# A macaron block (routed experts, diagonal state space, routed experts) on one core: a new middle stage and routing with one fp16 number

## The chip, the cores and the metric

The kernel runs on one NeuronCore of a Trainium2 chip. TensorE multiplies matrices into PSUM; VectorE, ScalarE and GpSimd do the elementwise work; SyncE issues most of the DMAs. TensorE's clock has two levels, 2.4 and 1.2 GHz, and the profile shows the granted one as a share of full speed. The metric is device microseconds of one execution.

## The reference

```python
# x: 4096 tokens of 256 numbers
x = x + 0.5 * ffn(layernorm(x))
x = x + ssm(layernorm(x))
x = x + 0.5 * ffn(layernorm(x))

def ffn(x):                          # 8 experts, hidden size 1024
    p = softmax(x @ Wr)              # the largest p chooses the expert
    h = gelu(x @ W1[e] + b1[e])      # erf form
    return max(p) * (h @ W2[e] + b2[e])

def ssm(u):                          # 128 complex states, diagonal
    h_t = a_disc * h_{t-1} + B_disc @ u_t
    return Re(C @ h_t)
```

## The kernel before

Everything stays on one core, and the engines are joined by semaphores; each engine's program is written out in its order. There are five stages.

Entry: x comes in as eight chunks of 512 tokens (4 tiles of 128 rows), row statistics are taken (`entry_stats`), the rows are transposed by TensorE and multiplied by the centred routing weights to give the logits. At the same time the 16 expert weight matrices are loaded and each is split into two fp16 parts; ScalarE sums the magnitudes (`row_sums`) and makes the high part, VectorE the scales (`weight_scales`) and the low part (`low_part`). Between these, VectorE's program has the steps of the first routing.

Routing (`route_*`): from the logits, VectorE finds each token's expert (`route_choose`), TensorE counts tokens before each one, VectorE turns this into a slot in a list sorted by expert (`route_count`), in tiles of 128 tokens of one expert, 39 tiles at most. `route_tiles` makes for each token a row over the tiles, once with the tile's start (GpSimd's `tile_starts`) and once with its partition, and `route_rows` a row over the 128 slots (32 operations of 128 columns). TensorE multiplies one with the other, which puts the number of the token into its slot, and `route_sorted` makes three index lists of it (`sorti`). `route_weigh` gives the largest probability, which goes to DRAM with mean and deviation as one record a token.

Experts (`ffn`, run twice): for each of 39 tiles GpSimd gathers rows and records by index, ScalarE normalises them (`norm`), TensorE transposes (`turn_tile`), VectorE splits them into a high and a low fp16 part (`split_x`), TensorE does the first product in three terms (`product1`), ScalarE does GELU, VectorE splits the result (`split_h`), TensorE does the second product (`product2`), VectorE scales it and adds x (`result`), and GpSimd scatters the rows.

Middle (state space): a loop over the eight chunks, with up to five of them in SBUF (XS). VectorE takes the statistics of the rows (`row_stats`, L580 to L586), GpSimd makes the inverse deviation, ScalarE normalises (L430), TensorE transposes (L976) and multiplies into the states (L1134), ScalarE copies the result (L543). The recurrence is a real scan after a rotation: VectorE multiplies by the cosine (L913), GpSimd by the sine (L414), VectorE runs two scans (L917, L920), and four one-column operations (L927 to L930) carry the state to the next chunk. GpSimd rotates back (L397, L399, L403), TensorE multiplies out of the states (L1114), and VectorE adds y to the rows (L942). Then for the next routing the new rows have statistics, a normalisation, transposes and logits of their own (L982), which trail the chunk loop: the logits of chunk c are copied LATE = 4 iterations later (L908).

Last come the second routing and the second expert stage. Two places of the code before:

```python
posi -> q1 = (iota_b == tile_b)                    # L749
dve.tensor_scalar(sval[:, :, 1, :], q1, part[:], None, ALU.mult)   # L752
...
last = dve.tensor_scalar(onerow[:, j, :], iota_b[:], slot_f[:, j:j + 1], None, ALU.is_equal)   # L757
```

## Time and profile before

| | |
|---|---|
| median of 3 runs | 737.88 us (733.58 to 748.28) |
| span of the profiled execution | 743.5 us |
| TensorE matmuls busy | 589.5 us (79%) |
| VectorE busy | 531.1 us (71%) |
| ScalarE busy | 396.8 us (53%) |
| GpSimd busy | 330.0 us (44%) |
| mean granted TensorE clock | 0.869 |

The profile is of one execution: the table gives for each engine the time in which it had an instruction in work. The only own time that the profiled execution has is its span, from the first to the last instruction; it lies within the spread of the runs and 5.6 us above their median. PE is TensorE's matmul, PEld its weight load, DVE VectorE, ACT ScalarE, POOL GpSimd, SP SyncE.

### The profile page before, as it was taken

How to read it: one execution, taken by the hardware profiler on the slowest of the kernel's cores; microseconds unless marked ns; L12 is line 12 of the kernel's file. 1: busy time of each engine (PE TensorE's matmuls, PEld its weight loads, DVE VectorE, ACT ScalarE, POOL GpSimd, SP SyncE). 2: the span in 40 equal slices, each digit the busy share in tenths (PEclk: the TensorE clock that was granted, in tenths of full speed). 3: DMA queues.
4: the chain of work that ended last, by engine and by line, in shares of the span. 5: the costliest groups of instructions: out<-in, count | busy, mean ns of one | idle time of the engine just before them, and what ended most of it. 6: DMA issues, size and time to landing. Idle time of an engine off the chain costs nothing.

```text
span 743.5 us, 18466 instructions
## 1 busy us (share of the span) xinstructions
PE 589.5 (79%) x6396; PEld 518.0 (70%) x6396; DVE 531.1 (71%) x1204; ACT 396.8 (53%) x879; POOL 330.0 (44%) x310
## 2 busy tenths in 40 slices
PE   5960149999999899994477878139999999999997
PEld 5950138998888787893245657129998778988886
DVE  5869967778886775784499993927776666766675
ACT  4877846565554555552336653107555546546463
POOL 0031183555545453531477881162555454554532
PEclk9555559999999999998658895558999999999999
DMA  8993031111111111113102211030111111111210
GB/s 276 374 375 122 5 99 31 40 45 43 49 45 38 35 51 37 38 30 99 51 29 90 80 57 57 1 103 19 44 51 44 36 50 36 45 41 36 50 36 2
DMA packets 34872, 51.86 MB, mean 70 GB/s; under 512 B 6747, under 2 KB 27933, under 8 KB 34528
## 3 DMA queue, kind: packets, MB, share of 16 engines
q1 hardware_dynamic: 24800, 31.90, 12.6%
q0 software_dynamic: 9984, 18.79, 9.0%
q8 instruction: 55, 0.90, 0.5%
q14 instruction: 33, 0.27, 0.1%
HBM read 37.95 MB, written 14.55 MB: 71 GB/s over the span
## 4 chain that ended last, share of the span: by engine, by line
PE 68%; DVE 18%; issue 7%; DMA 3%; ACT 2%; POOL 1%; SPq 1%; ACTq 0%; POOLq 0%; DVEq 0%
PE bank L1065 31%; PE bank L1082 9%; PE bank L1083 9%; PE bank L1084 9%; PE bank L982 4%; PE bank L1041 3%; DVE stats L580 3%; DVE weights_arena L613 2%; PE bank L976 2%; DMA weights_arena<-L_attn_u 2%; DVE weights_arena L920 1%; DVE weights_arena L757 1%; DVE weights_arena L917 1%; DVE weights_arena L942 1%; DVE ev L927 1%
## 5 line engine op out<-in xcount | busy, mean ns | idle before, releaser
L519 ACT ACTIVATE weights_arena<-bank,b1t,inv 128x128 f32<-128x128 f32 x624 | 228.4, 467 | 211.2 <-PE bank L1065 161.2
L1065 PE MATMUL bank<-weights_arena 128*128 128x128 f16 x3744 | 239.2, 222 | 23.5 <-issue 17.5
L1065 PEld LDWEIGHTS bank<-weights_arena 128*128 x3744 | 220.6, 99 | 39.8 <-issue 37.0
L1082 PE MATMUL bank<-weights_arena 128*128 x624 | 170.2, 273 | 1.2 <-issue 1.0
L1083 PE MATMUL bank<-weights_arena 128*128 x624 | 170.1, 273 | 1.3 <-issue 1.1
L1084 PE MATMUL bank<-weights_arena 128*128 x624 | 170.1, 273 | 0.9 <-issue 0.6
L816 DVE TENSOR_SCALAR weights_arena<-weights_arena,hscale 128x512 f16<-128x512 f32 x156 | 76.8, 492 | 83.6 <-ACT weights_arena L519 77.4
L819 DVE SCALAR_TENSOR_TENSOR weights_arena<-weights_arena,hscale 128x512 f16<-128x512 f32 x156 | 117.3, 752 | 5.6
L375 POOL DMA_INDIRECT recf<-records,sorti x78 | 81.4, 1043 | 23.8 <-issue 23.8
L381 POOL DMA_INDIRECT out<-weights_arena,sorti x39 | 39.5, 1013 | 112.7 <-DVE weights_arena L835 99.8
L381 POOL DMA_INDIRECT x_after_ffn<-weights_arena,sorti x39 | 40.6, 1040 | 105.3 <-DVE weights_arena L835 95.8
L1084 PEld LDWEIGHTS bank<-weights_arena 128*128 128x128 f16 x624 | 61.0, 98 | 10.5 <-issue 3.5
L1083 PEld LDWEIGHTS bank<-weights_arena 128*128 128x128 f16 x624 | 61.1, 98 | 9.0 <-issue 2.9
L1082 PEld LDWEIGHTS bank<-weights_arena 128*128 128x128 f16 x624 | 61.0, 98 | 8.9 <-issue 2.4
L803 DVE TENSOR_SCALAR weights_arena<-bank,xscale 128x256 f16<-128x256 f32 x78 | 37.7, 484 | 38.8 <-issue 17.2
L504 ACT ACTIVATE weights_arena<-weights_arena,recf 128x256 f32<-128x256 f32 x78 | 48.7, 626 | 30.1 <-DMA recf<-records,sorti 28.1
L375 POOL DMA_INDIRECT weights_arena<-L_attn_u,sorti x39 | 44.0, 1128 | 30.3 <-DVE sorti L788 18.8
L976 PE MATMUL bank<-ident,weights_arena 128*128 128x128 f32 x192 | 37.0, 358 | 19.6 <-ACT weights_arena L430 18.1
L976 PEld LDWEIGHTS bank<-ident,weights_arena 128*128 128x128 f32 x192 | 32.2, 195 | 27.5 <-ACT weights_arena L430 22.5
L832 DVE SCALAR_TENSOR_TENSOR weights_arena<-bank,inv,weights_arena 128x256 f32<-128x256 f32 x78 | 37.4, 479 | 19.1 <-PE bank L1084 9.5
L375 POOL DMA_INDIRECT weights_arena<-x_after_ssm,sorti x39 | 41.0, 1050 | 20.3 <-issue 11.6
L1041 PE MATMUL bank<-ident,weights_arena 128*128 128x128 f32 x156 | 31.4, 283 | 15.0 <-ACT weights_arena L504 13.1
(181 smaller groups left out, 702.0 us busy)
## 6 DMA issues: line engine op xcount, KB each, us to landing
weights_arena<-L_ffn_W SPq DMA_DIRECT2D x16, 1024.0 KB, 12.6
weights_arena<-L_attn_u SPq DMA_DIRECT2D x8, 512.0 KB, 9.9
weights_arena<-x_after_ffn SPq DMA_DIRECT2D x8, 512.0 KB, 4.8
x_after_ssm<-weights_arena SPq DMA_DIRECT2D x8, 512.0 KB, 3.1
weights_arena<-L_ffn_b SPq DMA_DIRECT2D x2, 1024.0 KB, 4.4
recf<-records,sorti POOLq DMA_INDIRECT x78
weights_arena<-L_attn_u,sorti POOLq DMA_INDIRECT x39
x_after_ffn<-weights_arena,sorti POOLq DMA_INDIRECT x39
```

The source lines that it names most:

```text
L375: pool.indirect_dma_start(to, None, source, bass.IndirectOffsetOnAxis(ap=sorti[:, q, index:index + 1].bitcast(U32), axis=0)).then_inc(s["g ...
L381: pool.indirect_dma_start(dst, bass.IndirectOffsetOnAxis(ap=sorti[:, q, 2:3].bitcast(U32), axis=0), og[q % 2], None, bounds_check=T - 1, o ...
L504: act.activation(xng[q % 2], xg[q % RING], ACT.Identity, bias=recf[:, q % RING, 0:1], scale=recf[:, q % RING, 1:2]).then_inc(s["xn"], 1)
L519: last = act.activation(hb[q % 2][:, f, :], src, ACT.Gelu, bias=b1t[:, bass.ds(e * FC + f, 1)], scale=inv1[:, bass.ds(e, 1)])
L816: dve.tensor_scalar(hs[q % 2][:, 0, f, :], hb[q % 2][:, f, :], sc, None, ALU.mult) \
L819: dve.scalar_tensor_tensor(hs[q % 2][:, 1, f, :], hb[q % 2][:, f, :], sc, hs[q % 2][:, 0, f, :], ALU.mult, ALU.subtract).then_inc(s["hspli ...
L976: last = pe.transpose(banks[d][:, i * P:(i + 1) * P], src[:, i, d * P:(d + 1) * P], ident[:])
L1041: last = pe.transpose(bank[6 + q % 2][:, d * P:(d + 1) * P], xng[q % 2][:, d * P:(d + 1) * P], ident[:])
L1065: last = pe.matmul(acc[:, f * P:(f + 1) * P], weights[wpart * DC + d], xts[q % 2][:, xpart, d, :], start=(n == 0), stop=(n == 5))
L1082: pe.matmul(acc, hs[q % 2][:, 0, f, :], high, start=(f == 0), stop=False)
L1083: pe.matmul(acc, hs[q % 2][:, 0, f, :], low, start=False, stop=False)
L1084: last = pe.matmul(acc, hs[q % 2][:, 1, f, :], high, start=False, stop=(f == FC - 1))
```

## The change

The middle stage and the routing are written anew; the expert stage changes in three places.

- The first expert stage takes mean and variance of each result row on VectorE and stores them behind the row: rows of 258 numbers (RW) in place of 256 in the buffer between.
- All eight chunks are loaded into SBUF at once. GpSimd makes the deviations in three batches, of chunk 0, of 1 and 2, and of 3 to 7; VectorE's loop begins when all three are ready.
- No products on GpSimd: VectorE multiplies both halves in one operation of 1024 columns, out of PSUM, runs both scans in place, and rotates back in one operation and a sum.
- Logits by linearity: the rows behind the state space are x + y, so the logits are those of the normalised x times its deviation, plus those of y, for which the matrix out of the states has nine more columns (eight experts and the mean). Normalisation, transposes and copies of the new rows go. ScalarE takes the new variance as a sum of squares; GpSimd makes its inverse square root at the end, for all 32 columns, and `route_odds` multiplies by it.
- Routing with one fp16 number: the number of the token, shifted by 2048 and never 0, in place of two bf16 numbers. One operation of 1280 elements multiplies it in, and `route_rows` is four operations of 1024, whose operands are laid out in pairs. The list for the first gather is released ahead of the other two.
- In the expert stage the high part of x is made by ScalarE, in the order GELU of q, high x of q+2, norm of q+3; TensorE's second product waits for `o_chain` in place of `o`.
- TensorE has extra products that nobody reads (`idle`) at the start of the middle and around the routing.

Not shown below: the layout of the buffers, the fp16 constants (token numbers), the nine columns of `ct` made at entry with one small product, the dropped operation and new order in `route_count`, and most of the removed lines.

```diff
-LATE = 4
-XS = 5
+PAIRS = 2
+RW = D + 2
...
-    x1_dram = nc.dram_tensor("x_after_ffn1", [T, D], F32, kind="Internal").ap()
+    x1_dram = nc.dram_tensor("x_after_ffn1", [T, RW], F32, kind="Internal").ap()
...
-            for c in range(XS):
-                sp.dma_start(xs[c], x1_chunks[c]).then_inc(sx[c], 16)
+            for c in range(NC):
+                sp.dma_start(xs[:, c * CT:(c + 1) * CT, :], x1_chunks[c]).then_inc(s_load[c], 16)
             for c in range(NC):
...
+            for first, last in BATCHES:
+                for c in range(first, last):
+                    pool.wait_ge(s_load[c], 16)
+                of = slice(first * CT, last * CT)
+                pool.tensor_scalar(nb[:, of], xs[:, of, D], -1.0, None, ALU.mult)
+                chain.link(pool.tensor_scalar(var1[:, of], xs[:, of, D + 1], EPS, None, ALU.add))
+                chain.link(pool.tensor_tensor(rs[:, of], var1[:, of], mhalf[:, of], ALU.pow))
+                chain.link(pool.tensor_tensor(sd[:, of], rs[:, of], var1[:, of], ALU.mult))
+                pool.tensor_tensor(nb[:, of], nb[:, of], rs[:, of], ALU.mult).then_inc(s_nb, 1)
+            pool.wait_ge(s_sq, NC)
+            chain.link(pool.tensor_scalar(m2[:], m2[:], 1.0 / D, EPS, ALU.mult, ALU.add))
+            chain.link(pool.tensor_tensor(rstd, m2[:], mhalf[:], ALU.pow))
+            pool.tensor_tensor(shift, nmean[:], rstd, ALU.mult).then_inc(s_nb2, 1)
...
+                def high_x(q):
+                    e = experts[q] = act.value_load(eid[0:1, q:q + 1], min_val=0, max_val=E - 1)
+                    act.wait_ge(s["turned"], q + 1)
+                    if q >= 2:
+                        act.wait_ge(s["xt"], q - 1)
+                        act.wait_ge(s["m1"], q * 2 - 2)
+                    src = bank[6 + q % 2][:, 0:DC * P].rearrange("p (c t) -> p c t", c=DC)
+                    act.activation(xts[q % 2][:, 0], src, ACT.Copy, scale=xscale[:, bass.ds(e, 1)]).then_inc(s["xt_hi"], 1)
                 norm(0)
                 norm(1)
+                high_x(0)
+                norm(2)
+                high_x(1)
                 for q in range(NT):
...
                         last.then_inc(s["gelu"], 1)
+                    if q + 2 < NT:
+                        high_x(q + 2)
+                    if q + 3 < NT:
+                        norm(q + 3)
...
+            def normalise(c):
+                act.wait_ge(s_nb, 1 + sum(first <= c for first, last in BATCHES[1:]))
                 if c >= 2:
+                    act.wait_ge(s_ut, c - 1)
+                for i in range(CT):
+                    j = c * CT + i
+                    act.activation(uns[c % 2][:, i, :], xs[:, j, 0:D], ACT.Identity, bias=nb[:, j:j + 1],
+                                   scale=rs[:, j:j + 1]).then_inc(s_un, 1)
+            def turned(c):
+                act.wait_ge(s_ut, c + 1)
                 if c >= 2:
+                    act.wait_ge(s_lg, c - 1)
+                for d in range(DC):
+                    last = act.copy(uts[c % 2][:, d, :], bank[d])
+                last.then_inc(s_uts, 1)
+            def squares(c):
+                act.wait_ge(s_x2, c + 1)
+                act.wait_ge(s_nm, c + 1)
+                if c >= 1:
+                    act.wait_ge(s_sq, c)
+                for i in range(CT):
+                    j = c * CT + i
+                    last = act.activation(dumps[i], xs[:, j, 0:D], ACT.Square, bias=nmean[:, j:j + 1],
+                                          accum_out=m2[:, j:j + 1])
+                last.then_inc(s_sq, 1)
...
+            def route_odds(ph):
+                s = S[ph]
+                dve.wait_ge(s["top"], 1)
+                dve.wait_ge(a_nb if ph == 1 else s_nb2, 1)
+                dve.tensor_tensor(je(rt[0]), je(rt[0]), over_e(rstd), ALU.mult).then_inc(s["diff"], 1)
...
+                dve.tensor_scalar(place_i[:, 0], posi, P - 1, None, ALU.bitwise_and)
+                link(dve.tensor_scalar(place_i[:, 1], posi, 7, None, ALU.arith_shift_right))
+                link(dve.tensor_copy(place_h, place_i.unsqueeze(3).to_broadcast([P, 2, NJ, PAIRS])))
+                pairs = lambda a: a.rearrange("p j (k t) -> p j k t", t=PAIRS)
+                link(dve.tensor_tensor(
+                    pairs(q1), iota_h[:, 0:NTE].rearrange("p (k t) -> p k t", t=PAIRS).unsqueeze(1)
+                    .to_broadcast([P, NJ, NTE // PAIRS, PAIRS]),
+                    place_h[:, 1].unsqueeze(2).to_broadcast([P, NJ, NTE // PAIRS, PAIRS]), ALU.is_equal))
+                dve.tensor_tensor(pairs(sval), pairs(q1),
+                                  token_h[:].unsqueeze(2).to_broadcast([P, NJ, NTE // PAIRS, PAIRS]), ALU.mult) \
+                    .then_inc(S[ph]["vals"], 1)
...
+                of = slice(GR * g, GR * g + GR)
+                dve.tensor_tensor(
+                    onerow[:, of, :].rearrange("p j (k t) -> p j k t", t=PAIRS),
+                    iota_h[:].rearrange("p (k t) -> p k t", t=PAIRS).unsqueeze(1).to_broadcast([P, GR, P // PAIRS, PAIRS]),
+                    place_h[:, 0, of, :].unsqueeze(2).to_broadcast([P, GR, P // PAIRS, PAIRS]), ALU.is_equal) \
+                    .then_inc(S[ph]["row"], 1)
...
+                number = bank[1][:, 0:NT]
+                upper, empty, token, high = (view(12928 + NTE * k, NT) for k in range(4))
+                dve.tensor_scalar(empty, number, 0.0, BIG, ALU.is_equal, ALU.mult)
+                link(dve.tensor_scalar(upper, number, 0.0, None, ALU.is_gt))
+                link(dve.tensor_tensor(token, number, upper, ALU.subtract))
+                link(dve.scalar_tensor_tensor(token, token, float(T // 2), empty, ALU.add, ALU.add))
+                dve.tensor_scalar(sorti[:, :, 0], token, float(T - 1), None, ALU.min).then_inc(s["sorted_sb"], 1)
+                dve.wait_ge(s["sorted_sb"], 1)
+                dve.tensor_scalar(sorti[:, :, 1], sorti[:, :, 0], P - 1, 5, ALU.bitwise_and, ALU.arith_shift_left)
+                dve.tensor_copy(sorti[:, :, 2], token)
+                link(dve.tensor_scalar(high.bitcast(I32), sorti[:, :, 0], 7, None, ALU.arith_shift_right))
+                dve.tensor_tensor(sorti[:, :, 1], sorti[:, :, 1], high.bitcast(I32), ALU.add).then_inc(s["sorted_all"], 1)
...
                     dve.wait_ge(s["o_chain"], q + 1)
+                    last = dve.scalar_tensor_tensor(o, o, recf[:, q % RING, 2:3], xg[q % RING], ALU.mult, ALU.add)
+                    if ph == 1:
+                        link(last)
+                        link(dve.bn_stats(stats[:, q % 2, :], o))
+                        last = dve.bn_aggr(og[q % 2][:, D:D + 2], stats[:, q % 2, :])
+                    last.then_inc(s["o"], 1)
...
+            def logits_of(c):
+                dve.wait_ge(s_y, c + 1)
+                of = slice(c * CT, (c + 1) * CT)
+                dve.scalar_tensor_tensor(nmean[:, of], ybanks[:, :, D + E], -1.0, xs[:, of, D], ALU.mult, ALU.subtract) \
+                    .then_inc(s_nm, 1)
+                link(dve.tensor_tensor(lpart[:], ybanks[:, :, D + NB:D + NB + E],
+                                       sd[:, of].unsqueeze(2).to_broadcast([P, CT, E]), ALU.mult))
+                dve.tensor_tensor(logits[:, of, :], lpart[:], ybanks[:, :, D:D + E], ALU.add).then_inc(s_lg, 1)
+            def add_y(c):
+                rows = xs[:, c * CT:(c + 1) * CT, 0:D]
+                dve.tensor_tensor(rows, rows, ybanks[:, :, 0:D], ALU.add).then_inc(s_x2, 1)
...
+            dve.wait_ge(s_nb, len(BATCHES))
+            for c in range(NC):
+                dve.wait_ge(s_g, c + 1)
+                dve.tensor_tensor(zz, turn[:], both(bank[2]), ALU.mult).then_inc(s_mod, 1)
+                dve.wait_ge(s_mod, c + 1)
+                for part_of in range(2):
+                    scan = dve.tensor_tensor_scan(zz[:, part_of, :], rho[:].to_broadcast([P, CH]), zz[:, part_of, :],
+                                                  state[:, part_of:part_of + 1], ALU.mult, ALU.add)
+                scan.then_inc(s_scan, 1)
+                if c >= 1:
+                    logits_of(c - 1)
+                    add_y(c - 1)
+                dve.wait_ge(s_scan, c + 1)
+                if c + 1 < NC:
                     dve.tensor_tensor(ev[:, 20:21], zi, sl, ALU.mult)
                     link(dve.tensor_tensor(ev[:, 21:22], zr, sl, ALU.mult))
...
+                    link(dve.scalar_tensor_tensor(state[:, 1:2], zi, cl, ev[:, 21:22], ALU.mult, ALU.subtract))
+                link(dve.tensor_tensor(zb, zz, back[:], ALU.mult))
+                if c >= 2:
+                    dve.wait_ge(s_y, c - 1)
+                dve.tensor_tensor(hr[c % 2], zb[:, 0, :], zb[:, 1, :], ALU.add).then_inc(s_hr, 1)
+            logits_of(NC - 1)
+            dve.wait_ge(s_lg, NC)
             route_choose(2)
+            add_y(NC - 1)
             route_count(2)
             route_tiles(2)
             for g in range(NJ // GR):
                 route_rows(2, g)
...
+                    for j in range(GR * g, GR * g + GR):
+                        last = pe.matmul(bank[1][:, 0:NTE], onerow[:, j, :], sval[:, j, :], start=(j == 0), stop=(j == NJ - 1))
                     last.then_inc(s["rowused"], 1)
...
+            def turn_chunk(c):
+                if c >= 1:
+                    pe.wait_ge(s_uts, c)
+                for i in range(CT):
+                    pe.wait_ge(s_un, c * CT + i + 1)
+                    for d in range(DC):
+                        last = pe.transpose(bank[d][:, i * P:(i + 1) * P], uns[c % 2][:, i, d * P:(d + 1) * P], ident[:])
+                last.then_inc(s_ut, 1)
+            def into_states(c):
+                pe.wait_ge(s_uts, c + 1)
+                if c >= 1:
+                    pe.wait_ge(s_mod, c)
+                for d in range(DC):
+                    last = pe.matmul(bank[2], bt[:, d, :], uts[c % 2][:, d, :], start=(d == 0), stop=(d == DC - 1))
+                last.then_inc(s_g, 1)
+            def out_of_states(c):
+                if c >= 1:
+                    pe.wait_ge(s_lg, c)
+                    pe.wait_ge(s_x2, c)
+                for i in range(CT):
+                    for d in range(DC):
+                        pe.matmul(ybanks[:, i, D + NB:D + NB + E], uts[c % 2][:, d, i * P:(i + 1) * P], wrc[:, d, 0:E],
+                                  start=(d == 0), stop=(d == DC - 1))
+                pe.wait_ge(s_hr, c + 1)
+                for i in range(CT):
+                    last = pe.matmul(ybanks[:, i, 0:D + NB], hr[c % 2][:, i * P:(i + 1) * P], ct[:], start=True, stop=True)
+                last.then_inc(s_y, 1)
+            idle(10, CH)
+            turn_chunk(0)
+            into_states(0)
+            turn_chunk(1)
+            for c in range(NC):
                 if c + 1 < NC:
...
+            idle(8)
             route(2)
             ffn(2)
```

## Rows read from the trace of the kernel before

**Rows 1.** Busy time by stage: stretch in us, length, engines, granted clock, DMA share, GB/s.

```profile
104.00:343.00 239.00, 226.41 (x2882) 205.12 (x2882) 172.93 (x350) 133.11 (x351) 113.57 (x110) 0.99 0.14 40
343.00:364.00 21.00, 6.38 (x16) 3.81 (x17) 4.81 (x22) 5.70 (x11) 3.62 (x6) 0.60 0.38 125
364.00:452.00 88.00, 66.38 (x297) 47.91 (x296) 82.43 (x211) 44.36 (x85) 66.37 (x58) 0.81 0.19 62
452.00:464.00 12.00, 9.33 (x44) 8.60 (x42) 1.31 (x11) 4.22 (x8) 1.22 (x2) 0.54 0.10 35
464.00:494.00 30.00, 5.43 (x40) 3.02 (x41) 21.16 (x75) 3.10 (x5) 8.63 (x8) 0.50 0.14 51
494.00:743.50 249.50, 229.85 (x2882) 207.25 (x2880) 165.85 (x310) 131.86 (x349) 112.86 (x111) 0.98 0.13 38
```

**Rows 2.** Timeline of one iteration of the middle: start us, duration us, engine, line.

```profile
394.99 1.96 PE L1114 MATMUL bank<-ct,weights_arena 128*128 128x256 f32 x8 [1.87 <-DVE weights_arena L942]
...
396.88 0.68 DVE L913 TENSOR_TENSOR weights_arena<-weights_arena,turn 128x512 f32<-128x512 f32 x1
...
397.31 1.09 PE L976 MATMUL bank<-ident,weights_arena 128*128 128x128 f32 x8 [0.36 <-ACT weights_arena L430]
...
398.24 1.85 PE L982 MATMUL bank<-wr,weights_arena 128*128 128x8 f32 x16
398.44 1.07 ACT L530 COPY weights_arena<-bank 128x512 f32<-128x512 f32 x2 [1.18 <-PE bank L976]
...
398.80 1.26 DVE L920 TENSOR_TENSOR_SCAN weights_arena<-rho,state,weights_arena 128x512 f32<-128x512 f32 x1
398.96 2.16 POOL L397 TENSOR_TENSOR weights_arena<-weights_arena,back 128x512 f32<-128x512 f32 x1
...
399.95 1.96 PE L1134 MATMUL bank<-weights_arena,bt 128*128 128x512 f32 x4
400.16 0.98 DVE L927 TENSOR_TENSOR ev<-weights_arena,turn 128x1 f32<-128x1 f32 x1
...
401.06 0.15 DVE L928 TENSOR_TENSOR ev<-weights_arena,turn 128x1 f32<-128x1 f32 x1
...
404.41 1.28 DVE L942 TENSOR_TENSOR weights_arena<-weights_arena,bank 128x512 f32<-128x512 f32 x2
```

**Rows 3.** The lower clock: one timeline row, and a stretch of two microseconds.

```profile
379.79 3.78 PE L1134 MATMUL bank<-weights_arena,bt 128*128 128x512 f32 x4 [1.16 <-ACT weights_arena L530]
...
404.00:406.00 2.00, 0.16 (x1) 0.19 (x2) 1.93 (x9) 0.00 (x0) 1.27 (x3) 0.78 0.00 0
```

**Rows 4.** Load of the middle's rows, first statistics, and GpSimd's power at entry.

```profile
350.00:352.00 2.00, 0.00 (x0) 0.00 (x0) 1.20 (x4) 0.00 (x0) 0.00 (x0) 0.50 1.07 367
...
350.80 1.40 DVE L580 BATCH_NORM_STATS2 stats<-weights_arena 128x6 f32<-128x256 f32 x4 [6.91 <-DMA weights_arena<-x_after_ffn]
...
36.39 7.50 POOL L353 TENSOR_TENSOR records<-weights_arena,mhalf 128x32 f32<-128x32 f32 x1 [19.39 <-DVE weights_arena L865]
```

**Rows 5.** Timeline of the second routing, VectorE.

```profile
473.21 1.49 DVE L749 TENSOR_TENSOR weights_arena<-iota_b,weights_arena 128x1280 bf16<-128x1280 bf16 x1
474.74 2.72 DVE L752 TENSOR_SCALAR weights_arena<-weights_arena,part 128x1280 bf16<-128x1280 bf16 x1
...
477.38 5.29 DVE L757 TENSOR_SCALAR weights_arena<-iota_b,weights_arena 128x128 bf16<-128x128 bf16 x32
...
485.40 0.18 DVE L788 TENSOR_SCALAR sorti<-weights_arena 128x39 int32<-128x39 f32 x1
```

**Rows 6.** Waits at entry (60 to 104): total us, times, longest.

```profile
ACT weights_arena L459 <- DVE wscale L606: 7.2, 3, 3.3
```

**Rows 7.** Waits in the first experts (130 to 340), and two rows of their timeline.

```profile
PE bank L1065 <- DVE weights_arena L805: 1.8, 2, 1.5
...
303.03 2.90 ACT L519 ACTIVATE weights_arena<-bank,b1t,inv 128x128 f32<-128x128 f32 x8 [3.74 <-PE bank L1065]
...
312.26 0.94 PE L1065 MATMUL bank<-weights_arena 128*128 128x128 f16 x14
```

384 lines of the change are left out of this document (109 added, 275 removed).

## The prediction

> **What bounds the kernel now.** The span is 743.5 us, the median of the three runs 737.9 (733.6 to 748.3), so I subtract from 743.5 and take the 5.6 us between span and median off at the end. I read the stretches by stage first [rows 1]. The two expert stages (104 to 343 and 494 to 743.5) have TensorE busy 226 of 239 and 230 of 249.5 us at the high clock: TensorE sets them. The middle stage, from 343 until the logits are complete at 464, is 121 us, and the second routing, until the first product at 494, is 30. From 364 to 452 VectorE is busy 82 of 88 us while TensorE has 66 and ScalarE 44: eight iterations, one per chunk, of 11 us. After it come 12 us in which TensorE works alone through two late chunks of transposes and logits, because they trail by LATE = 4. Then I followed one iteration in the timeline [rows 2]. VectorE's one-column products cost 0.98 us (L927) and 0.15 (L928): the long one starts at 400.16 and ends when GpSimd's product L397, begun at 398.96, has ended (401.12). So two of VectorE's four state operations (L927, L929) wait about a microsecond each for GpSimd. In the routing I look at what follows what: TensorE and ScalarE are nearly idle, VectorE goes from one operation to the next, and the clock is at its lower level.
>
> **The iteration of the middle, anew.** VectorE per chunk, at the durations of [rows 2]: multiply with PSUM, 1024 columns, 1.2 (L942 takes 1.28 for two of 512); two scans 2.5 (twice L920's 1.26); three short ones for mean and logits 0.5 (each like L928 with its wait); adding y 1.2 (as L942); four state operations 0.65 without GpSimd; the backward product of 1024 columns 1.25 and the sum of 512 0.65 (L913: 0.68 for 512). Sum 7.95, with the waits between them 8.1, against 11. Gone are both statistics (2 x 2 us: L580 and what follows it) and the two waits for GpSimd; GpSimd's products come in.
> But the change also ties a ring. The copy of chunk c+2 out of PSUM (ScalarE, 1.07, L530) now waits for the logits of chunk c, since TensorE's logits read that buffer. Behind it on TensorE, in order: into states 1.96 (L1134), transposes 1.09 (L976), eight logit products 0.93 (half of L982's 1.85), y 2.03 (L1114's 1.96 for 265 columns in place of 256), then VectorE's 0.5. With 0.3 for handing over that makes 7.9 us at the high clock: just hidden under 8.1. At the low clock the same terms are 3.78 (L1134 in [rows 3]) and twice the others: 13.3 us, longer than the old iteration. The old clock fell in the gaps (404 to 406: 0.78) though TensorE was busy 66 of 88 us, and its mean was 0.81, that is 38% of the time low. TensorE's new share is 6.0 of 8.1 us, as full as before (7.9 of 11), with a gap of some 2 us in each iteration. Bounds 8.1 and 13.3; mixed by time (62% and 38%), 9.5 us. As a ring at the low clock keeps TensorE busy 11.5 of 13.3 us, which ought to raise the clock again, I take 8.9.
>
> **The start of the middle.** The last tile of the first expert stage gains a row statistic behind its result (L580: 0.35 a row, plus aggregate and waits): +0.6 until its scatter. The first chunk, which VectorE had at 350.80, comes at 351.4; the other seven of 528 KB, 3.7 MB, take 10.1 at the 367 GB/s of the old load [rows 4]: complete at 361.5. SyncE issues all eight in a row, and its stores stand behind them; the first of these is wanted 20 us later. I keep up to 370 for the high end, as rows of 1032 bytes move at a rate that no row shows. GpSimd's third batch needs all of them: pow costs 7.50 us for 32 columns (L353), 0.234 each, so 4.7 for 20 columns, plus four short operations with waits, 1.2: about 367 to 368. VectorE now waits for this batch before its first multiply (the old loop began at 364); behind that wait stand all of its chunk work, and behind that the second product into the states. TensorE's ten idle products after the last tile (5 us at most) end before the first transposes can come; they hide in the load. First multiply 368, first iteration without logits 6.1, six at 8.9: the last begins at 427.5; 7.4 until its sum, y at 2 to 3.9, logits 0.5: 438.4 against 464. **The middle gives 25.5 us.** The tail is where most is won: the old logits came some 25 us after the last chunk's multiply, the new ones by 11.
>
> The Trainium skill (DMA: Bandwidth & Descriptors, How a descriptor splits into AXI transactions) says that a transfer not starting on a 256-byte boundary also fetches the bytes below its start. A row of 1032 bytes would then fetch 128 bytes more on average, and the estimate of the seven chunks' load by this page is 11.4 us for 10.1. No row of before shows such a transfer.
>
> **The routing.** From 464 to the sorted list at 485.6 [rows 5] it takes 21.7 us. Choose stays; y's last add (1.2) now stands between choice and counts, of which 0.8 was spare: +0.4. Count loses one 256-column operation: -0.5. In tiles, L752 took 2.72 us for 1280 elements, beside GpSimd's product for the tile starts; both go. The two new operations over 1280 fp16 elements take L749's 1.49 each, or about 0.8 if pairs of 16-bit elements pass two at a time (the same slope halved, above the 0.15 of L928). Tiles: 5.2 before, 3.9 or 2.5 after. Rows: 32 operations in 5.29 before, four of 1024 elements after, 1.2 or 0.7 each: 4.8 or 2.8. Odds +0.45; sorted lists -0.1 to the first gather (its other indices, 0.7, hide behind that gather's issue). A new wait: the odds need the variances. ScalarE's last squares (four of about 0.6) start behind y's add, then GpSimd takes 0.3 + 7.5 + 0.3, ready 15 us after the logits; VectorE is there after 13.5 in the fast case, 16.9 in the slow one. Behind the wait stand odds, owners, weights and the sorted list. So 18.5 or 20.6 for 21.7. No row shows a two-operand 16-bit operation with both inputs in steps of one (L749 repeats one of them), so I keep both ends. I take the fast one, as L757 already handles 128 16-bit elements in 0.165 us, where L749's slope would give 0.28: **-3.2**. On GpSimd the gathers now stand behind the variances (ready at 15 us), before the sorted list at 18.5 that they need anyway.
> The Trainium skill (VectorE: DVE Perf Modes, the perf-mode tier table) gives tensor_tensor two 16-bit elements a cycle with unit steps and one otherwise; L749 at 1.49 fits the latter, and its rule makes the routing 18.5, without it 20.6.
>
> **Entry.** In the first routing the same VectorE operations stand in the way of the weight scales: ScalarE waited 7.2 us for L606 in three waits, the longest 3.3 [rows 6]; tiles stand before one of them and rows before the next. The savings on VectorE (0.5 + 1.3 to 2.7 + 0.5 to 2.5) come out there as far as these idle times reach: 2 to 5, I take **-3**. The new constants and the extra product for the readout fall before the second x chunks land, in VectorE's idle time.
>
> **Expert stages.** High x moves from VectorE (0.48) to ScalarE, which is busy 133 of 239 us; the statistics add 0.45 and two waits on VectorE in the first stage (173 of 239). With it go the waits for transposes and products and the register load. ScalarE now makes it behind GELU of q, and norm q+3 is queued behind it. A tile takes 6.1 us (239 / 39). GELU of one tile ran from 303.03 to 305.93, and TensorE began the first product of the tile two later at 312.26 [rows 7]. High x at 305.93 takes 0.5; VectorE's low part at worst comes behind the second half of the split of h, the result and its statistics, at 309.3: 2.9 us to spare. TensorE waited for L805 only 1.8 us in all of 130 to 340 [rows 7]. Nothing, then; range -4 to +4 over both. At each start high x now stands behind the second norm: +0.2.
>
> **Sum.** -25.5 - 3.2 - 3 + 0.4 for the two starts: 31.3 off 743.5 is 712.2, less 5.6: **706 us**, 4.3% faster. A measurement of this kernel tells about 2% from no change.
>
> **Rivals.**
> A, the clock stays up in the loop: 8.1 an iteration, 5 us less, with entry at its best 2 more and the load at its earliest: 697. For it: TensorE's gaps shrink from up to 3 us to 2; against it: the old loop was as full and fell.
> B, the ring at the low clock is the bound for most of the loop: 13.3 for six iterations is 26 more, 732; for half of them 719. For it the old mean of 0.81, against it that a bound TensorE is a busy one. At the high end this is no change by 2%.
> C, the first multiply waits for slow rows of 1032 bytes or for pow beside VectorE: +3 to +10, 709 to 716.
> D, slower: the hand-over of x in the experts. ScalarE's high x sits behind GELU, TensorE's next first product behind it. It costs nothing until the 2.9 us to spare are used; beyond that each microsecond is paid on 78 tiles. At 1.0 over, 706 + 78 = 784; from 0.4 over the kernel is slower than before, from 0.6 by over 2%. For it only that first tiles have no lead; against it [rows 7] and ScalarE's 106 idle us.
> E, the multiplies without GpSimd don't lose the wait in L927 (it was something else): two microseconds more for seven iterations, 720. The times of L397 speak against it.
>
> **How the numbers follow.** Forecast 0.56 (698 to 715), A 0.14, C 0.10, B at half 0.09, B in full 0.06, E 0.02, D 0.03. The range 692 to 724 holds the forecast, A, C, E and B at half: it leaves out D, full B and the ends of the expert stages' uncertainty. Faster by over 2% means below 723: all but D, B in full and a part of B at half and C: 0.88; same 0.09; slower 0.03.
>
> **What would show it.** Right: L913's successor every 8 to 9.5 us, all state operations at 0.15 to 0.2, first multiply near 368, logits complete near 438, scan-to-logit tail of 11, the 1280-element multiplies at 0.8 and the 1024-element compares at 0.7, expert stages of 239 and 249. Wrong: iterations of 11 to 13 with TensorE continuously busy (B), a first multiply after 371 (C), TensorE waiting for low x in the experts (D), a wait before the odds of more than 2 us.

## The result, and the profile after

The kernel after takes 681.9 us (median of four runs, 676.3 to 684.2), the kernel before 736.4 beside it (734 to 748): ratio 0.923, 95% interval 0.917 to 0.929. I had forecast 706, in a range that ended at 692. The profiled execution has a span of 679.9 us and took 681.7.

First the stages, as in [rows 1] (stretch, length, busy us and count of PE, weight loads, VectorE, ScalarE and GpSimd, granted clock, DMA share, GB/s). The six stretches are: first experts; last product to first multiply; the loop; its tail to the logits; routing; second experts.

```profile
100.00:332.50 232.50, 223.67 (x2881) 206.86 (x2881) 178.75 (x387) 149.96 (x389) 109.59 (x109) 0.99 0.15 41
332.50:357.00 24.50, 15.96 (x44) 7.31 (x41) 1.60 (x5) 8.14 (x16) 11.04 (x17) 0.83 0.54 173
357.00:413.40 56.40, 44.53 (x226) 31.81 (x226) 51.50 (x87) 26.39 (x73) 0.00 (x0) 0.92 0.16 56
413.40:424.80 11.40, 9.25 (x51) 7.96 (x52) 7.43 (x13) 3.85 (x16) 0.00 (x0) 0.85 0.14 48
424.80:450.00 25.20, 12.78 (x106) 10.69 (x104) 16.47 (x48) 5.65 (x14) 13.14 (x10) 0.82 0.25 82
450.00:680.00 230.00, 222.01 (x2882) 208.13 (x2882) 150.71 (x272) 147.24 (x387) 107.81 (x111) 0.98 0.15 41
```

From span to span 63.6 us are gone. Taking each stage from the start of its first product to that of its last three, by the instruction rows: 4.1 before the first product, 5.7 in the first experts (238.2 to 232.5), 33.8 in middle and second routing (151.6 to 117.8), 19.8 in the second experts (243.9 to 224.1). My sum had 31.3 in all and nothing in the experts.

One iteration on VectorE, in answer to [rows 2]. The four state operations (L926 to L929) take 0.15 to 0.22, with no long one among them. VectorE waits for y (L901), 1.13 here and about 0.4 later. The multiplies (L915) follow one another by 6.3, 8.6, 8.9 and then 8.2 us.

```profile
371.86 1.22 DVE L915 TENSOR_TENSOR weights_arena<-turn,banks 128x1024 f32<-128x1024 f32 x1 [0.88 <-PE banks L1119]
373.12 2.46 DVE L918 TENSOR_TENSOR_SCAN weights_arena<-rho,state,weights_arena 128x512 f32<-128x512 f32 x2
376.71 0.16 DVE L901 SCALAR_TENSOR_TENSOR nmean<-banks,weights_arena 128x4 f32<-128x4 f32 x1 [1.13 <-PE banks L1133]
...
378.24 0.15 DVE L926 TENSOR_TENSOR ev<-weights_arena,turn 128x1 f32<-128x1 f32 x1
378.31 0.15 DVE L927 TENSOR_TENSOR ev<-weights_arena,turn 128x1 f32<-128x1 f32 x1
...
380.75 1.22 DVE L915 TENSOR_TENSOR weights_arena<-turn,banks 128x1024 f32<-128x1024 f32 x1
```

The start of the middle, as in [rows 4]: GpSimd has the last load at 352.06, and its power of 20 columns takes 3.56 where I had 4.7. The first multiply follows at 356.98.

```profile
352.06 0.29 POOL L377 TENSOR_SCALAR nb<-weights_arena 128x20 f32<-128x20 f32 x1 [4.60 <-DMA weights_arena<-x_after_ffn]
352.42 0.28 POOL L378 TENSOR_SCALAR var<-weights_arena 128x20 f32<-128x20 f32 x1
352.78 3.56 POOL L379 TENSOR_TENSOR rs<-var,mhalf 128x20 f32<-128x20 f32 x1
```

The second routing, as in [rows 5]: 0.83 and 0.82 for the two operations over 1280 elements, 2.56 for all rows, and L698 behind them without an idle time in brackets, so nothing waits for the variances.

```profile
433.64 0.83 DVE L729 TENSOR_TENSOR weights_arena<-iota_h,weights_arena 128x1280 f16<-128x1280 f16 x1
434.50 0.82 DVE L733 TENSOR_TENSOR weights_arena<-weights_arena,token_h 128x1280 f16<-128x1280 f16 x1
435.25 2.56 DVE L740 TENSOR_TENSOR weights_arena<-iota_h,weights_arena 128x1024 f16<-128x1024 f16 x4
437.73 0.41 DVE L698 TENSOR_TENSOR weights_arena<-weights_arena,records 128x256 f32<-128x256 f32 x1
```

And the tail, still partly at the lower clock [rows 3]: the last chunk's logit products and y.

```profile
414.60 2.03 PE L1133 MATMUL banks<-ct,weights_arena 128*128 128x265 f32 x8
418.78 2.17 PE L1129 MATMUL banks<-wrc,weights_arena 128*128 128x8 f32 x16 [2.15 <-DVE weights_arena L910]
420.80 3.46 PE L1133 MATMUL banks<-ct,weights_arena 128*128 128x265 f32 x8
```

### The profile page after: what moved, and what is told of

Read it like the earlier page. It is cut to its first block, busy times and chain, and to the rows that moved or that the text cites. A ratio compares the mean times of both kernels' runs of the same rounds, so it can differ in the third digit from the quotient of the medians.

```text
span 679.9 us, 18383 instructions
## 1 busy us (share of the span) xinstructions
PE 576.7 (85%) x6428; PEld 518.4 (76%) x6428; DVE 483.6 (71%) x1015; ACT 416.1 (61%) x965; POOL 262.7 (39%) x263
## 4 chain that ended last, share of the span: by engine, by line
PE 69%; DVE 11%; issue 11%; DMA 3%; POOL 2%; ACT 1%; SPq 1%; DVEq 1%; ACTq 0%; POOLq 0%
PE banks L1060 30%; PE banks L1079 9%; PE banks L1077 9%; PE banks L1078 9%; PE banks L1036 2%; PE banks L1133 2%; PE banks L1119 2%; PE banks L1129 2%; DMA weights_arena<-x_after_ffn 1%; POOL records L336 1%; DVE weights_arena L918 1%; PE banks L965 1%; PE banks L993 1%; DVE weights_arena L573 1%; SPq L312 1%
## 5 line engine op out<-in xcount | busy, mean ns | idle before, releaser
L490 ACT ACTIVATE weights_arena<-banks,b1t,inv 128x128 f32<-128x128 f32 x624 | 226.2, 468 | 44.1 <-PE banks L1060 24.5
L1060 PE MATMUL banks<-weights_arena 128*128 128x128 f16 x3744 | 236.3, 222 | 12.8 <-issue 9.0
L1060 PEld LDWEIGHTS banks<-weights_arena 128*128 x3744 | 221.6, 99 | 23.0 <-issue 19.2
L1077 PE MATMUL banks<-weights_arena 128*128 x624 | 170.6, 273 | 0.0
L1078 PE MATMUL banks<-weights_arena 128*128 x624 | 170.5, 273 | 0.0
L1079 PE MATMUL banks<-weights_arena 128*128 x624 | 170.5, 273 | 0.0
L475 ACT ACTIVATE weights_arena<-banks,xscale 128x256 f16<-128x256 f32 x78 | 37.0, 474 | 110.0 <-PE banks L1036 74.8
L791 DVE SCALAR_TENSOR_TENSOR weights_arena<-banks,xscale,weights_arena 128x256 f16<-128x256 f32 x78 | 37.7, 484 | 45.8 <-issue 30.8
L1079 PEld LDWEIGHTS banks<-weights_arena 128*128 128x128 f16 x624 | 61.2, 98 | 7.3
L1077 PEld LDWEIGHTS banks<-weights_arena 128*128 128x128 f16 x624 | 61.2, 98 | 6.6
L1078 PEld LDWEIGHTS banks<-weights_arena 128*128 128x128 f16 x624 | 61.2, 98 | 6.4
L818 DVE SCALAR_TENSOR_TENSOR weights_arena<-banks,inv,weights_arena 128x256 f32<-128x256 f32 x78 | 37.5, 480 | 13.7 <-PE banks L1079 10.8
L594 DVE SCALAR_TENSOR_TENSOR weights_arena<-weights_arena,wscale 128x2048 f16<-128x2048 f32 x16 | 37.4, 2345 | 5.5 <-ACT weights_arena L417 5.4
L1036 PE MATMUL banks<-ident,weights_arena 128*128 128x128 f32 x156 | 30.7, 280 | 11.0 <-ACT weights_arena L462 9.9
```

Of the source, the lines that this page charges most:

```text
L490: last = act.activation(hb[q % 2][:, f, :], src, ACT.Gelu, bias=b1t[:, bass.ds(e * FC + f, 1)], scale=inv1[:, bass.ds(e, 1)])
L791: dve.scalar_tensor_tensor(xts[q % 2][:, 1], src, sc, xts[q % 2][:, 0], ALU.mult, ALU.subtract) \
L1036: last = pe.transpose(bank[6 + q % 2][:, d * P:(d + 1) * P], xng[q % 2][:, d * P:(d + 1) * P], ident[:])
L1060: last = pe.matmul(acc[:, f * P:(f + 1) * P], weights[wpart * DC + d], xts[q % 2][:, xpart, d, :], start=(n == 0), stop=(n == 5))
L1077: pe.matmul(acc, hs[q % 2][:, 0, f, :], high, start=(f == 0), stop=False)
L1078: pe.matmul(acc, hs[q % 2][:, 0, f, :], low, start=False, stop=False)
```

## The experiments

Each set of kernels ran on another chip, and the kernel before ran beside each: 723, 743, 738, 701 and 702 us. So a ratio to before compares within a chip, and the stages below, of one profiled execution each, help to explain it. The executions of e5 and e12 took 5 and 7 us more than the medians of their kernels. For each profiled execution: before's median on its chip; first product; first experts; last product to the first of the second stage; second experts. In brackets are TensorE's gaps: between two products of one half tile (24 of the first product, 12 of the second), where neither waits for a semaphore, the distance beyond the usual 0.056 or 0.109 us, where that is over 0.12, summed from the instruction rows.

```
                 before  first   experts 1     middle+   experts 2
                         product               routing
before             736   104.0  238.2 (15.4)   151.6   243.9 (18.1)
after              736    99.9  232.5 (13.2)   117.8   224.1 ( 2.7)
e1_experts         723   105.0  232.7 ( 8.5)   152.2   222.2 ( 2.0)
e2_experts_back    723   100.1  237.7 ( 7.6)   117.3   221.6 ( 3.0)
e3_norm_order      723   104.1  228.6 ( 7.7)   151.9   224.8 ( 4.2)
e4_no_idle         723    99.7  228.0 ( 8.7)   118.0   225.5 ( 3.1)
e5_before_again    743   105.6  240.4 (13.8)   154.1   240.8 (14.6)
e6_after_again     743    97.6  232.2 (13.0)   118.0   231.0 ( 8.4)
e7_unpaired        743   103.2  231.6 (13.3)   121.3   227.7 ( 6.3)
e8_early           743    97.5  231.8 (13.1)   111.8   225.5 ( 3.4)
e9_experts2        738   105.0  245.1 (19.3)   151.9   226.4 ( 4.1)
e10_norm2          738   105.6  233.8 (11.4)   154.2   234.9 ( 9.8)
e11_back2          738    97.5  238.8 ( 9.0)   117.3   245.5 (17.4)
e12_pad            738   103.2  242.4 (15.5)   151.7   242.0 (18.6)
e13_fewer          701   105.4  219.8 ( 0  )   153.3   216.2 ( 0  )
e14_more           701    99.9  219.6 ( 0  )   120.5   216.9 ( 0  )
e15_high_x         701    97.6  233.8 ( 0  )   115.1   215.8 ( 0  )
e16_best           701    99.6  219.0 ( 0  )   109.0   217.2 ( 0  )
e17_fewer2         702   105.5  219.6 ( 0  )   153.7   215.9 ( 0  )
e18_more2          702   105.5  219.3 ( 0  )   156.2   216.3 ( 0  )
```

**The expert stages' edits alone, and put back.** e1 and e9 are the same kernel, the kernel before with this edit (`high_x`, ScalarE's split, is defined as in the change above):

```diff
                 norm(1)
+                high_x(0)
+                norm(2)
+                high_x(1)
                 for q in range(NT):
-                    if q + 2 < NT:
-                        norm(q + 2)
 ...
                         last.then_inc(s["gelu"], 1)
+                    if q + 2 < NT:
+                        high_x(q + 2)
+                    if q + 3 < NT:
+                        norm(q + 3)
 ...
-                    dve.tensor_scalar(xts[q % 2][:, 0], src, sc, None, ALU.mult).then_inc(s["xt_hi"], 1)
 ...
-                        pe.wait_ge(s["o"], q - 1)
+                        pe.wait_ge(s["o_chain"], q - 1)
```

e2 and e11 are the kernel after with this diff reversed.

> The kernel before with the expert stages' edits of the change alone: high x on ScalarE behind GELU of q, norm of q+3 behind it, the second product waiting for VectorE's first of two operations on the result. Theory S (the unforeseen 24 us of the two expert stages come from these edits): the stages fall from 238 and 250 to about 233 and 231, the time by 20 to 24 us, to about 714. Rival R (they come from elsewhere: the clock at which the second stage starts, the code of the other stages, the data layout): at most 4 us of the stages move, 732 to 738.

> The kernel before with the expert stages' edits of the change alone, a second time. On the chip where before takes 722 us it brought 0.5%, the expert stages being near 233 and 222 us with or without it. On the chips where before takes 736 to 743, its expert stages have 14 to 18 us each of gaps between products that wait for no semaphore (in after: 13 and 3 to 8). Theory I (such gaps are TensorE's supply of instructions, tied to a place in the program and to the chip, not to the order of ScalarE's and VectorE's work): on such a chip the edit alone leaves the gaps of before in place, gain under 1.5%. Theory S (the late split takes TensorE's lead and so makes it feel the supply): the gaps or their cost fall, gain 2.5 to 3.3%.

> The kernel after with its expert stages put back: high x on VectorE, norm of q+2 ahead of GELU of q, the second product waiting for the finished result. Theory S: about 20 to 24 us more than after, 702 to 706, the second stage back near 250. Rival R: within 4 us of after, 678 to 686. If the row statistics behind the result hurt when they stand ahead of the product's wait, the first stage alone would be longer than 238.

> The kernel after with its expert stages' orders put back, a second time. Theory I: the ratio to before stays where the middle, the routing and the position of the code put it, within 1% of after's 0.922. Theory S: 0.95 or more, the second stage near 240.

Edits alone: 0.9947 of before (0.990 to 1.000) on the chip of 723, 0.9926 (0.988 to 0.997) on that of 738. Put back in after: 0.948 (0.945 to 0.952), 7.8 us above e4 on the same chip, and 0.951 (0.942 to 0.961), against 0.923 and 0.922 for after itself on other chips. The second stages of the chips at 736 to 743 are the clear reading: with the old order 243.9, 240.8, 242.0 and 245.5 us, with the new one 224.1, 231.0, 227.7, 225.5 and 226.4. The edit is worth 10 to 20 us in that stage there, in the kernel before too. But the whole of e9 gains only 5 us on its chip, and its first stage, 245.1, gives some of the rest back (two tiles of 12.0 and 10.8 us, with gaps of 3.9 and 3.8). On the chip of 723 the second stage is 222 to 226 in either order. Where ScalarE waited in the second stage (total, times, longest): first GELU in before and in e11_back2, then high x (L475) and GELU (L490) in after, then GELU in e13_fewer (old order, chip of 701):

```profile
ACT weights_arena L519 <- PE bank L1065: 78.2, 32, 4.0
ACT weights_arena L519 <- remote: 29.8, 11, 7.6
```

```profile
ACT weights_arena L477 <- PE banks L1047: 78.5, 33, 3.8
ACT weights_arena L477 <- remote: 31.1, 11, 7.5
```

```profile
ACT weights_arena L475 <- PE banks L1036: 33.5, 23, 2.3
ACT weights_arena L475 <- remote: 29.0, 13, 2.5
ACT weights_arena L490 <- remote: 6.8, 1, 6.8
ACT weights_arena L490 <- PE banks L1060: 4.3, 5, 2.4
```

```profile
ACT weights_arena L519 <- PE bank L1065: 83.6, 39, 3.9
```

The waits for the product are the ordinary lead of ScalarE; those put down to "remote" follow no product that had just ended. At GELU there are 11 of them with the old order, one with the new, none on the chip without gaps. They don't vanish with the new order: 13 of them, 29.0 us, now stand at high x, which ScalarE makes two tiles ahead. So the edit may pay because a late start now falls where a tile has time to spare; no run shows that, nor which of the three parts of the edit does it.

**The norm's order alone, and the place of the code.** e3 and e10 move only `norm(q + 2)` from ahead of GELU of q to `norm(q + 3)` behind it, in the kernel before. e12 adds to before, behind its first `ffn(1)` on TensorE,

```diff
+            for _ in range(24):
+                pe.matmul(bank[2][:, 0:P], ident[:], turn[:, 0, 0:P], start=True, stop=True)
```

> The kernel before with one thing changed: ScalarE normalises tile q+3 behind GELU of tile q, where it normalised q+2 ahead of it. Theory S1 (a late GELU is what costs, because a norm that waits for its gather or transposes stands ahead of it): most of the 20 us, 716 to 720. Theory S2 (VectorE's load is what costs, and high x must leave it): less than 5 us, 731 to 738.

> The kernel before with norm of q+3 behind GELU of q, a second time. Its TensorE program is that of before, instruction for instruction. Theory I: on a chip where before takes 736 to 743 the same gaps stand at the same tiles as in before (stage 2: 14, 17, 21, 28, 32) and the gain is under 1%. Theory S: tile times fall to 5.5 to 5.9 us and the gain is 2 to 3%.

> The kernel before with 24 idle products (48 weight loads and 48 products in TensorE's program) behind the first expert stage, where TensorE waits some 15 us for its next work, so that they cost nothing by themselves; they move all later code of TensorE by some 100 instructions. Theory I: the first expert stage is as before; in the second the gaps stand at other tiles, and their sum may go either way (by up to 12 us). Rival: the gaps of the second stage stand at the same tiles, so the place of TensorE's code is not what sets them.

The norm's order: 0.997 (0.994 to 1.000) and 1.002 (0.998 to 1.007), nothing. The profiled execution on the chip of 738 has a shorter second stage (234.9), but it was among the fastest three of ten, and the median shows no gain. The shifted code: 1.000 (0.994 to 1.005); long tiles stand at 14, 17 and 21 of the second stage as in before, others have moved. That speaks against the place of TensorE's code as their cause.

**Both kernels again on one chip.**

> The kernel before itself, unchanged, profiled on the chip of this job. In the job before this one its median was 723 us where the first comparison had 736, and two kernels with other orders in the expert stages stood at 720 to 722. Theory N (the unforeseen gain of the expert stages is no effect of the edits: the same instructions of before take a different time there from one chip to the next): its two expert stages are near 230 and 225 here, as in those two kernels, where the profile shown had 238 and 244. Theory S (the old order is slower by itself): 238 and 244 again. Where this program is slow, tiles of 5.6 us alternate with tiles of over 6.

> The kernel after itself, unchanged, on the same chip. Middle stage and second routing together, last product to first, 118 us as in its profile; expert stages about 228 to 232 and 222 to 225. Theory N: 676 to 682, ratio to before 0.935 to 0.95 in place of 0.923. Theory S: ratio 0.923 again.

Before 743.5, after 685.4, ratio 0.922 (0.915 to 0.930): the first result repeats. Theory N fell on this chip: 240.4 and 240.8. (On the chip of 723 it held, as e2 and e4 show for the second stage: 221.6 with the old order, 225.5 with the new.)

**Idle products.** e4 deletes the four `idle(...)` calls of after.

> The kernel after without TensorE's idle products, at the start and end of the middle stage and in the second routing. My reading of after: the 8.8 us of idle products after the first expert stage end before the loads have come, so they delay nothing; without them the first iterations, the tail and the first tiles of the second expert stage run at the low clock: 3 to 8 us more, 685 to 690. Rival: they bring nothing, since the clock falls while the first multiply is awaited anyway: within 2 us. Rival R's form for the expert stage: the second stage loses its gain of 19 us, 700.

0.935 (0.931 to 0.939), 678.7 us, so not the 3 to 8 us more that I expected. After itself was not timed on this chip, but middle and routing are 118.0 in its profile too: idle products bring nothing that can be seen where they stand. In both kernels the first multiply follows GpSimd's last batch, so a faster first product into the states can't show.

**Pairs.** e7 changes one line of after.

```diff
-PAIRS = 2
+PAIRS = 1
```

> The kernel after with PAIRS = 1: the fp16 operands of the routing are repeated element by element and no longer in pairs, nothing else. Theory: pairs are what lets VectorE pass two a cycle. Then the two operations over 1280 elements go from 0.83 to about 1.5 and the rows from 2.5 to 4.3 each four; per routing 1.3 + 1.8 = 3.1 or more, in the second all of it on the path, in the first most of it in front of the weight scales: 4 to 7 us more than after. Rival: the layout makes no difference to the rate: within 1 us.

0.934 (0.927 to 0.941), 6.4 us more than after on the same chip. By the profiles it is 5.6 more at entry and 3.3 more in the routing, and 3.9 less in the experts, which the edit doesn't touch. The same operations as above:

```profile
436.21 1.49 DVE L729 TENSOR_TENSOR weights_arena<-iota_h,weights_arena 128x1280 f16<-128x1280 f16 x1
437.74 1.49 DVE L733 TENSOR_TENSOR weights_arena<-weights_arena,token_h 128x1280 f16<-128x1280 f16 x1
439.15 4.69 DVE L740 TENSOR_TENSOR weights_arena<-iota_h,weights_arena 128x1024 f16<-128x1024 f16 x4
```

**An earlier start of the loop, and a version that beats both.** e8 moves a wait of after; e16 is e8 with idle products where the clock was low.

```diff
-            dve.wait_ge(s_nb, len(BATCHES))
 ...
             def logits_of(c):
+                dve.wait_ge(s_nb, 1 + sum(first <= c for first, last in BATCHES[1:]))
```

```diff
-            idle(10, CH)
+            idle(13, CH)
 ...
             def out_of_states(c):
+                if c == NC - 1:
+                    pe.wait_ge(s_mod, NC)
+                    idle(10)
```

> The kernel after, with VectorE's one wait for all three batches of the row scales taken from ahead of the first multiply and put, batch by batch, ahead of the logits that read them. In after the first multiply stands at 357.0, while the first product into the states is ready about 10 us earlier. Theory L (this wait is worth its length): the first multiply comes at about 347, the loop ends 7 to 10 us earlier, 672 to 675 where after has 680 to 682. Rival P (GpSimd's pow and VectorE slow one another, or the ring of chunk 3 waits for its load and scales anyway): the early iterations take 2 to 4 us longer and the gain is 2 us or less.

> The kernel after with VectorE's early start of e8_early, with 13 idle products in place of 10 ahead of the middle stage (so that they end where the first transposes can begin) and ten more ahead of the last chunk's products, where the clock is low in after: into the states 1.4 us, logits and y of the last chunk up to 3 us sooner than in e8_early. 668 to 674, ratio 0.905 to 0.91. Rival: the clock stays low in these places whatever is put into the gaps: the same as e8_early, 0.911.

e8: 674.9 us, 0.911 (0.904 to 0.919), 10.5 us faster than after on the same chip, 6.2 of them in the middle. The rest lies in the second experts (225.5 for 231.0), which the edit doesn't touch. Its first multiply no longer waits for GpSimd; first after, then e8:

```profile
356.98 1.22 DVE L915 TENSOR_TENSOR weights_arena<-turn,banks 128x1024 f32<-128x1024 f32 x1 [22.29 <-POOL nb L381]
```

```profile
347.73 1.22 DVE L915 TENSOR_TENSOR weights_arena<-turn,banks 128x1024 f32<-128x1024 f32 x1 [16.08 <-PE banks L1119]
```

e16: 650.8 us, 0.928 (0.923 to 0.932), on the chip where before takes 701, so its expected ratio, made for the other chips, can't be compared. Middle and routing are 109.0, 2.8 less than e8's on another chip: 1.4 less before the first multiply and 3.1 less behind the last, but 1.7 more in the loop between. The first product into the states and the tail now run at the higher clock (1.98 where after had 3.78; y 2.04 where it had 3.46):

```profile
333.68 1.98 PE L1119 MATMUL banks<-weights_arena,bt 128*128 128x512 f32 x4 [1.16 <-ACT weights_arena L516]
...
397.86 1.92 PE L1132 MATMUL banks<-wrc,weights_arena 128*128 128x8 f32 x16
399.64 2.04 PE L1136 MATMUL banks<-ct,weights_arena 128*128 128x265 f32 x8
```

**High x alone, beside the statistics.** e15 is after with high x back on VectorE; the norm's new order and `o_chain` stay.

> The kernel after with high x alone back on VectorE; ScalarE still normalises q+3 behind GELU of q, and the second product still waits for the first operation of the result. If moving high x off VectorE is what counts: most of the 21 us of the whole expert edit, 696 to 704 (ratio 0.945 or more). If the earlier wait of the second product counts: within 4 us of after (ratio 0.92 to 0.93).

671.3 us, 0.960 (0.955 to 0.966), on a chip without gaps, beside e14 at 0.950. Its second stage is 215.8, but its first 233.8 in place of 219.6: VectorE (the third busy figure) is then busy 195.6 of 233.8 us, and tiles 10 to 18 take 6.4 to 7.6 us. First e15, then e16:

```profile
97.30:331.10 233.80, 220.78 (x2877) 203.85 (x2878) 195.58 (x424) 133.69 (x351) 108.94 (x109) 0.99 0.15 41
```

```profile
99.70:318.70 219.00, 216.69 (x2880) 204.83 (x2881) 178.13 (x387) 150.47 (x389) 110.15 (x109) 1.00 0.16 44
```

So the statistics would have cost 14 us in this stage if high x had not left VectorE. (e15's entry is 2 us shorter than e14's and its middle 3 us shorter than after's; no row says why.) It fits e2, whose first stage is 9.7 longer than e4's on the same chip.

**GpSimd's indirect DMAs.** In before a gap looks like this (PE, ScalarE and GpSimd rows of the second stage):

```profile
600.09 1.10 POOL L375 DMA_INDIRECT recf<-records,sorti  x1 [0.30 <-issue]
600.35 0.45 PE L1065 MATMUL bank<-weights_arena 128*128 128x128 f16 x5 [0.36 <-issue]
600.48 1.50 ACT L519 ACTIVATE weights_arena<-bank,b1t,inv 128x128 f32<-128x128 f32 x4 [1.58 <-remote]
601.12 0.33 PE L1065 MATMUL bank<-weights_arena 128*128 128x128 f16 x3 [0.32 <-issue]
601.86 1.56 PE L1065 MATMUL bank<-weights_arena 128*128 128x128 f16 x25 [0.41 <-issue]
```

and in after, in the first stage:

```profile
221.25 0.94 POOL L355 DMA_INDIRECT recf<-records,sorti  x1 [0.30 <-issue]
...
222.99 0.27 PE L1060 MATMUL banks<-weights_arena 128*128 128x128 f16 x2 [0.40 <-issue]
...
223.23 0.46 ACT L490 ACTIVATE weights_arena<-banks,b1t,inv 128x128 f32<-128x128 f32 x1 [2.13 <-remote]
```

TensorE goes on 1.77 and 1.74 us after the start of the DMA. Over both stages 33 of after's 42 gaps (e6: 37 of 48, before: 31 of 83, e1: 5 of 23) end 1.60 to 1.85 us after the start of GpSimd's latest indirect DMA; ends spread evenly over the stages would fall there about once in 25. So many gaps go with these DMAs, but in before and e1 most don't. e13 and e17 are before with `[0:3 - ph]` behind fetch's tuple of tables, e14 (after) and e18 (before) have a second `(recx[:, k, :], rec_dram[ph], 1)` in it for ph 2, with the counts of the waits to match.

> The kernel before, its second expert stage without the gathers of the tiles' records (it works with the records that the first stage left, so its numbers are not the reference's): GpSimd issues two indirect DMAs for a tile in place of three. Theory G (the gaps of TensorE, and late waits of the other engines, come while GpSimd issues indirect DMAs): on a chip where before takes 736 to 743 the second stage falls from 242 by 6 to 15 us, its gaps without a semaphore from 14 to 18 us to under 10. Rival I (instruction supply by place of the code): nothing but the wait for the first tile's record, 0 to 2 us.

> The kernel before without the record gathers of the second expert stage (it works with the records that the first stage left), a second time. Where the job's time of before is 736 us or more: theory G (the gaps come while GpSimd issues indirect DMAs) gives a second stage with less than 10 us of gaps and 6 to 15 us shorter than the 242 of before; theory I (the supply of the chip, whatever GpSimd does) gives 14 to 18 us of gaps again and a stage within 3 us. Where before takes about 701 us there are no gaps to be changed, and the stage is 216 as in e13_fewer.

> The kernel after with the record gather of each tile of the second stage issued twice, the second time into a buffer that nobody reads: four indirect DMAs for a tile. GpSimd is busy about 3 us of 5.6 per tile and would be 4. Theory G: gaps in the second stage grow from 3 to 8 us to 8 to 15, the stage by 4 to 12 us. Rival I: within 2 us of after.

> The kernel before with the record gather of the second expert stage issued twice, four indirect DMAs for a tile. Where the job's time of before is 736 us or more: theory G gives more gaps, 20 us or more, and a stage of 248 or more; theory I the 242 of before within 3 us. Where before takes about 701 us: 216 to 217, since 4 us of issuing fit into a tile of 5.5.

Both sets fell on chips without a gap, where the tiles take 5.52 whatever GpSimd issues. 1.009 and 1.007 for e13 and e17, 1.010 for e18, 0.950 for e14; e18 and e14 start their second stage some 2.5 us later, with six more DMAs to issue first. At the end e13 and e17 take 12 us, and e14 and e18 take 9, from the last product to the end of the span in place of 5.7, though the last scatter's packets land 2 us after its issue; no row tells why. Whether these DMAs set the gaps on the other chips was not tried there and stays open.

## Why the prediction was wrong

The step that failed is "Expert stages": "Nothing, then; range -4 to +4 over both". Measured: 25.5 us in the first pair of profiles (5.7 and 19.8), 18 in the second. I had read "TensorE busy 226 of 239" [rows 1] as TensorE setting the stage and took 239/39 = 6.1 us for what a tile takes. A tile without a gap takes 5.52 us in every trace (48 products at 0.056, 24 at 0.109, two transposes at 0.109), so 39 are 215 us: before loses 23 in its first stage and 29 in its second, and there was something to win, 46 us by the stages of the chips without gaps. The profile of before had it. Its page has "issue" at 7% of the chain, and 37.0 us of idle time put down to it ahead of the first product's weight loads:

```profile
L1065 PEld LDWEIGHTS bank<-weights_arena 128*128 x3744 | 220.6, 99 | 39.8 <-issue 37.0
```

Its waits have "remote" at GELU, 22.3 us in ten waits from 520 to 740. The 1.8 us of waiting for x and the 2.9 to spare [rows 7] were right, but I asked only whether the move could cost something. What the edit is worth depends on the chip: 10 to 20 us in the second stage where before takes 736 to 743, nothing at 723 and 701 in that stage, and at 701 14 in the first, but only to pay for the statistics. Why it brings that much where there are gaps stays open. Rival D priced the same edit, with the wrong sign.

On the chips of 701 and 702 both stages are 216 to 220 in before and after's kin alike, as the step said. There e14, which is after with one gather more, takes 34.7 us less than before. After itself was not timed there; without e14's 2.5 us ahead of the second stage and 3.4 at the end I estimate 41 us less, ratio 0.942. My working had 31.3, ratio 0.957 with the forecast of 706: what remains there are the misses of middle, routing and entry below.

"The middle gives 25.5 us": 29.0 (from the last product 92.3 where before had 121.3). First multiply 24.5 after that product, forecast 25: load complete a microsecond later than I had, pow 1.1 shorter. The seven chunks behind the first landed within 10.5 us (341.5 to 352.06), near the 10.1 of the old rate. The Trainium skill (DMA: Bandwidth & Descriptors, How a descriptor splits into AXI transactions) says that a transfer which does not start on a 256-byte boundary also fetches the bytes below its start. By my estimate from it these loads take 11.4; the trace shows less than half of that surplus. The loop is where the size was off: from the second multiply on 8.4 an iteration, forecast 8.9. The clock stayed higher than I had assumed (mean 0.92, for 0.81 in the old loop), which is close to rival A's 8.1, and y became VectorE's wait. My ring at the low clock was also added up wrongly: its terms give 13.7, not 13.3, and the mix 9.6, not 9.5. Tail 11.4, forecast 10.9. State operations as forecast, so E falls; B and C didn't come. The price of late scales was real, though: e8 shows 6.2 us for VectorE's one wait, which I counted as given and didn't test against a wait for each batch.

"Routing -3.2": -5.4 (16.3 for 21.7). The fast case came, and e7 shows that pairs make it. The wait of 1.5 us that I had for the variances did not come, as the last pow took 5.46 for 32 columns where [rows 4] had 7.50; without it my own terms give 5.0. By e7 the unpaired routing costs 3.3 more. The Trainium skill (VectorE: DVE Perf Modes, "Side-by-side: where the cycles go for N=2048 bf16" and the perf-mode tier table) gives tensor_tensor two 16-bit elements a cycle with unit steps and one otherwise; these runs agree with both halves, 0.83 paired and 1.49 unpaired.

"Entry -3": -4.1, and -8.0 on the chip of 743, of which e7 puts 5.6 on the pairs. ScalarE's waits for the scales [rows 6] were the right place to look.

"Idle products": I had 5 us at most, they take 8.8, and still end ahead of the first transposes, as forecast. "Less 5.6": not a constant. After's profiled run took 1.8 us more than its own span; the 5.6 belonged to one execution of before and didn't carry over.

## What to carry to other kernels

Work out what one tile takes when nothing disturbs it and multiply, before calling a stage bound by an engine that is busy 95%: the rest was 52 us here. Moving work off the fuller of the engines that feed TensorE changed nothing in a stage on one chip and was worth 10 to 20 us in it on others, and it was what made an addition next to it free (14 us). An edit timed on one chip alone says little of the next. Where a loop waits at its head for all batches of something, let each step wait for its own batch: that gave 6 us here.

## What the runs showed of the hardware

The kernel before takes 701, 702, 723, 736, 738 and 743 us in six sets of runs, and the difference lies in the expert stages (436 us for both without gaps, 482 with). The gaps come to 0 to 34 us and strike the same tiles of before on two chips (14, 17 and 21 of the second stage; tile 14 takes 8.15 and 8.16 us). They wait for no semaphore; instructions do come by DMA, as the third part of before's page counts them (packets, MB, share), but no run here ties these packets to the gaps:

```profile
q8 instruction: 55, 0.90, 0.5%
```

GpSimd's pow takes 1.04, 1.66, 3.56 and 5.46 us for 4, 8, 20 and 32 columns, and 7.50 for 32 at before's entry. A short operation of GpSimd's took longer beside VectorE: L377 over 20 columns takes 0.29 in after, where VectorE stands idle, 1.23 in e8 beside VectorE's scans, and 1.11 in e16. The pow behind it takes 3.56 in all three.

```profile
348.99 2.46 DVE L918 TENSOR_TENSOR_SCAN weights_arena<-rho,state,weights_arena 128x512 f32<-128x512 f32 x2
349.14 1.23 POOL L377 TENSOR_SCALAR nb<-weights_arena 128x20 f32<-128x20 f32 x1 [4.59 <-DMA weights_arena<-x_after_ffn]
```
